# P V of eight head pairs gathered into five blocks per batch, with one copy per block

## The reference, cut to what matters

```python
# x: [32, 256, 128]; 16 heads of 64, 4 persistent key/value rows per head
x = x + attn(layernorm(x))          # rms_norm, q k v, rope, causal softmax, w_out
x = x + ffn(layernorm(x))           # a gated recurrence over the 32 batches, then tanh
# the part of attn around the change:
scores = einsum('bhid,bhjd->bhij', q, k) * scale
attn = softmax(where(causal, scores, min), axis=-1)
out = einsum('bhij,bhjd->bhid', attn, v)     # the product "P V"
out = out.transpose(0, 2, 1, 3).reshape(b, n, heads * dim_head) @ w_out.T
```

## Time and profile before

| | us |
|---|---|
| median of 3 runs | 1124.64 |
| lowest, highest | 1124.19, 1130.9 |
| the profiled execution's own time | 1127.17 |
| its span, first to last instruction | 1125.4 |

### The profile page before, as it was taken

The page is one execution under the profiler, slowest core; times in us unless marked ns, Lnnn a source line. Parts: engine busy times, 40 slices in busy tenths (PEclk is TensorE's granted clock), DMA queues, the critical chain, the costliest instruction groups (busy, mean ns, idle before and its releaser), DMA issues.

```text
span 1125.4 us, 47265 instructions
## 1 busy us (share of the span) xinstructions
PE 1079.8 (96%) x18443; PEld 814.4 (72%) x18443; DVE 934.1 (83%) x3306; ACT 698.1 (62%) x1575; POOL 633.8 (56%) x819
## 2 busy tenths in 40 slices
PE   4979999999999999999999999999999999999996
PEld 2557777777777777777777777777777777777775
DVE  6778888888888888888888888888887889888645
ACT  3746665666666666666666666566675666666634
POOL 4546565556656555665565576565566566656510
PEclk8989999999999999999999999999999999999998
DMA  6222433432333333233333333333332333333215
GB/s 208 105 85 88 115 112 110 120 115 86 95 112 115 116 115 116 78 103 111 116 116 115 108 96 92 111 112 111 115 98 87 113 109 110 111 111 103 71 23 150
DMA packets 78031, 120.52 MB, mean 107 GB/s; under 512 B 13041, under 2 KB 35954, under 8 KB 77682
## 3 DMA queue, kind: packets, MB, share of 16 engines
q1 hardware_dynamic: 68714, 111.20, 32.4%
q10 hardware_dynamic: 9096, 6.30, 2.2%
HBM read 41.56 MB, written 8.78 MB: 45 GB/s over the span
## 4 chain that ended last, share of the span: by engine, by line
PE 66%; DVE 14%; DMA 10%; SPq 3%; issue 3%; POOL 1%; ACT 1%; DVEq 0%; POOLq 0%; ACTq 0%
PE bank_pv L1173 12%; PE bank L1065 12%; PE bank_st L1129 9%; DMA rope_c<-rope_b 7%; PE bank_sum L1210 6%; PE bank_sum L1194 5%; PE bank_sm L1104 4%; DVE masked L835 4%; PE bank L1087 4%; DMA linv_scratch<-linv 3%; PE bank L1084 2%; PE bank L1312 2%; PE bank L1314 2%; PE bank_st L1133 2%; SPq L312 2%
## 5 line engine op out<-in xcount | busy, mean ns | idle before, releaser
L419 POOL TENSOR_TENSOR qk<-rope_a,rope_c 128x512 f32<-128x512 f32 x256 | 341.0, 1332 | 301.2 <-DMA rope_c<-rope_b 293.4
L835 DVE CUSTOM_DVE_ANT_0 masked<-bank_sm,mask_q 128x132 bf16<-128x132 f32 (+1 forms) x1024 | 307.1, 354 | 16.5 <-PE bank_sm L1104 15.7
L412 POOL TENSOR_TENSOR prob<-prob 128x264 f32<-128x264 f32 x256 | 209.5, 818 | 120.0 <-ACT prob L559 113.4
L824 DVE TENSOR_TENSOR rope_a<-bank,cos 128x512 f32<-128x512 f32 x256 | 174.0, 680 | 121.5 <-PE bank L1065 80.7
L544 ACT ACTIVATE qk_h<-qk 128x512 f16<-128x512 f32 x256 | 160.4, 626 | 167.9 <-POOL qk L419 167.2
L559 ACT ACTIVATE prob<-bank_st 128x784 f32<-128x784 f32 x256 | 209.0, 817 | 60.3 <-PE bank_st L1138 59.6
L1173 PE MATMUL bank_pv<-prob,v_sb 128*64 128x256 f32 (+1 forms) x2048 | 224.7, 340 | 0.8 <-DVE raw L851 0.6
L1129 PE MATMUL bank_st<-qk 64*64 64x256 f32 (+3 forms) x4096 | 186.2, 299 | 0.2
L1129 PEld LDWEIGHTS bank_st<-qk 64*64 64x64 f32 x4096 | 167.7, 134 | 9.2 <-issue 0.9
L825 DVE TENSOR_TENSOR rope_b<-bank,sin 128x512 f32<-128x512 f32 x256 | 173.7, 679 | 0.0
L1173 PEld LDWEIGHTS bank_pv<-prob,v_sb 128*64 128x64 f32 x2048 | 124.3, 136 | 54.6 <-issue 1.3
(11 more groups left out here) (241 smaller groups left out, 1738.1 us busy)
## 6 DMA issues: line engine op xcount, KB each, us to landing
rope_c<-rope_b SPq DMA_DIRECT2D x512, 128.0 KB, 2.4
rinv<-linv_scratch SPq DMA_DIRECT2D x124, 256.0 KB, 4.7
out<-x_sb SPq DMA_DIRECT2D x16, 256.0 KB, 3.7
linv_scratch<-linv SPq DMA_DIRECT2D x62, 64.0 KB, 2.0
x_sb<-x ACTq DMA_DIRECT2D x28, 128.0 KB, 5.4
xt<-w_qkv_t ACTq DMA_DIRECT2D x1, 1024.0 KB, 5.4
v_end<-v_end_scratch SPq DMA_DIRECT2D x64, 8.0 KB
v_sb<-pm_v SPq DMA_DIRECT2D x63, 8.0 KB
```

What stands on the lines that cost most here:

```text
L412: G.tensor_tensor(prob_2[:, s % 4, :, :], prob[:, s % 4, :, 0:NT - Q1], prob[:, s % 4, :, C0 + Q1:SCOL], ALU.add).then_inc(S["prob_added"], 1)
L419: G.tensor_tensor(qk[:, s, :].rearrange("p (u n) -> p u n", u=2)[:, :, 0:NT], rope_a[:, (NPAIR * j + s) % 3, :].rearrange("p (u n) -> p u ...
L824: V.tensor_tensor(rope_a[:, (NPAIR * j + s) % 3, :], proj_bank(j, s)[:, :], cos[:, :], ALU.mult)
L835: ins = V.tensor_tensor_reduce(masked[:, e, c0:c0 + n], ps_sm[:, e, c0:c0 + n], mask_q[:, c0:c0 + n], 1.0, LOWEST, ALU.add, ALU.max, top[: ...
```

## The change

P V of a batch is done in five blocks instead of eight. Step 0 has pair 7 with the tail keys, step 2 pairs 0 and 1, step 4 pairs 2 and 3, step 5 pair 4, step 7 pairs 5 and 6. The second pair of a block goes into columns 256 to 511 of the same bank. Only the first pair of a block waits for the copies before it, and ACT makes one copy per block, of 512 or 256 columns. Steps 1, 3 and 6 have no P V any more.

```diff
+PV_AT = {0: (7,), 2: (0, 1), 4: (2, 3), 5: (4,), 7: (5, 6)}
...
-            def raw_copy(bj, par, s):
-                act.wait_ge(S["pv_ready"], NPAIR * bj + s + 1)
+            def raw_copy(bj, par, pairs_of):
+                s, n = pairs_of[0], len(pairs_of)
+                act.wait_ge(S["pv_ready"], NPAIR * bj + s + n)
...
-                A.activation(raw[:, par, s, :], ps_pv[:, 0:NT], ACT.Copy, scale=1.0 / RS).then_inc(S["raw_done"], 1)
+                A.activation(raw[:, par, s:s + n, :].rearrange("p s q -> p (s q)"), ps_pv[:, 0:n * NT], ACT.Copy,
+                             scale=1.0 / RS).then_inc(S["raw_done"], n)
...
                     if s == 0 and c:
-                        raw_copy(j - 2, p, NPAIR - 1)
+                        raw_copy(j - 2, p, PV_AT[0])
...
-                    if s >= 1 and b:
-                        raw_copy(j - 1, 1 - p, s - 1)
+                    if s in (2, 4, 5, 7) and b:
+                        raw_copy(j - 1, 1 - p, PV_AT[s])
...
-            def attend(bj, s):
+            def attend(bj, s, at):
                 pe.wait_ge(S["exp_done"], NPAIR * bj + s + 1)
 
-                wait(pe, S["raw_done"], NPAIR * bj + s)
+                if at == 0:
+                    wait(pe, S["raw_done"], NPAIR * bj + s)
...
-                        last = T.matmul(ps_pv[OWN[e], q0:NT], v_sb[:, kc, col:col + DH], prob[:, s % 4, e, c0:c0 + NT - q0],
+                        last = T.matmul(ps_pv[OWN[e], at + q0:at + NT], v_sb[:, kc, col:col + DH], prob[:, s % 4, e, c0:c0 + NT - q0],
...
                     if s == 0 and c:
-                        attend(j - 2, NPAIR - 1)
-                    if s >= 1 and b:
-                        attend(j - 1, s - 1)
+                        attend(j - 2, NPAIR - 1, 0)
+                    if s in (2, 4, 5, 7) and b:
+                        for i, pair in enumerate(PV_AT[s]):
+                            attend(j - 1, pair, i * NT)
```

## The result

The changed kernel takes 1141.97 us (median; 1141.72 to 1144.06), the kernel before 1127.66 in the four runs beside it. The ratio is 1.0132, 95% interval 1.0089 to 1.0174: slower by a little over one per cent. The prediction was 1142.2 us, 1.56% over the 1124.64 that it started from.

The account below looks back on a forecast made before the run. PE's work seemed the bound, with transpositions waiting for DVE's maxima and the DMA loop only 0.07 us from binding. 0 - 0.07 + 0.65 = +0.58 us per batch, 31 times, less 0.4, gave 1142.2 us; range 1133 to 1150.

Parts of the forecast that it names:

- The step that decided it: Before step 7's transposition: PE, without P V of pair 5, waits 0.8 us uncovered for DVE's maxima of pair 3.
- A second pair at 0.65 us: In a joined P V block: the second pair costs 0.65 us, where a block alone costs 0.81.
- Step 1 to step 3, nothing: From step 1's scores to step 3's transposition: DVE makes these 5.75 us, so joining pairs 0 and 1 changes 0.
- Step 3 to step 7, -0.07: Between the transpositions of steps 3 and 7: joining pairs 2 and 3 saves 0.16, the DMA loop passes only 0.07 us.
- Step 7 to step 1, +0.65: From step 7's transposition to the next step 1's scores: PE bounds these 9.82 us; pair 5's P V adds 0.65.
- The sum: Whole run: +0.58 us per batch, 31 times, with -0.4 for the last batch: +17.6 us, median 1142.2, 1.6% slower.
- The clock: PE's clock through the changed kernel: stays at 1.00 throughout despite a wait of 0.8 us in step 7.
- Faster (1109): Rival, whole kernel: PE's own work is the bound, three joins over 32 batches save 15.4 us; 1109 us, chance 6%.
- About the same (1131): Rival: step 7's 0.8 us wait is real but joins count in full, +0.22 per batch; 1131 us, chance 12%.
- A second pair at 0.81 (1150): Rival, joined P V blocks: a second pair costs as much as a first, 0.81 us; 1150 us, chance 10%.

## Why the prediction was right

**The step that decided it.** "Without the block PE is there at about 588.0 and stands until 588.76, a wait of 0.8 us with no cover": measured 0.73 us, 1.83 us behind the scores as before. The run with pair 5 back removed the loss and the run with pair 5's move alone had all of it.

**A second pair at 0.65 us.** Measured 0.66. Three passages into and out of the 128*64 shape less per batch do save 0.16 us each of PE's own work. The Trainium skill ("TensorEngine Tiling (Array Packing)", "Key Properties") says that a change of the tiling mode drains the engine; if nothing else had changed, the time should have fallen. The trace agrees with the rule, about 0.16 us for coming in and going out together. But pair 5's own 0.66 us went behind a wait that did not get shorter.

**Step 1 to step 3, nothing.** 5.75 us before and after. The join of pairs 0 and 1 turned into 0.19 us of idle PE before the transposition of step 3, where it had been 0.04.

**Step 3 to step 7, -0.07.** This term was sized too small: undisturbed batches took the whole 0.16 us (17.04 to 16.88). The mean over iterations 3 to 31 fell by 0.18, from 17.40 to 17.22. I had let only 0.07 through, from the one batch of the earlier trace rows, and in other batches the exchange lands earlier: from the rotation of pair 5 to the transposition, 11 of the 14 undisturbed batches have 7.4 to 7.9 us, where that batch has 7.35 and DVE's work takes 7.28.

**Step 7 to step 1, +0.65.** Measured 10.39, where from the transposition's start to the scores' start it had been 588.76 to 598.51, or 9.75; the means over iterations 3 to 30 are 10.40 and 9.75, so +0.65.

**The sum.** +0.58 a batch was forecast. Undisturbed batches went from 32.52 to 33.02 between last maxima, +0.50; over iterations 3 to 31 the mean grew by 0.47, or 13.6 us. The forecast has 16.8 for these 29, so it was 3.2 too high there, and nearly all of that is the term from step 3 to step 7 (0.11 a batch). The span grew by 16.9, which seems to agree with the 17.6, but 3.0 of it lie ahead of iteration 3, where the forecast has 0.6. The 2.4 beyond that are not the edit's, as far as the traces tell. In this execution the clock granted to PE rose later than in the one of before, with PE about as busy in the first stretch (5.31 and 5.29 us of 6.00). Stretches of both, the changed kernel first:

```profile
30.00:36.00 6.00, 5.31 (x29) 2.40 (x29) 4.46 (x20) 2.20 (x7) 2.30 (x2) 0.50 0.18 69
36.00:44.00 8.00, 7.61 (x128) 5.10 (x129) 6.35 (x26) 4.69 (x10) 4.15 (x5) 0.82 0.18 68
...
30.00:36.00 6.00, 5.29 (x34) 2.48 (x32) 4.97 (x22) 2.84 (x8) 2.11 (x2) 0.74 0.20 76
36.00:44.00 8.00, 7.89 (x167) 5.74 (x167) 7.26 (x34) 5.61 (x11) 6.29 (x10) 1.00 0.22 82
```

A clock of 0.50 is the lower of PE's two levels, 1.2 GHz, and 1.00 the upper, 2.4 GHz. From the first transposition of step 7 to the scores of the next step 1 PE took 8.57 us in this execution and 6.29 before. The run with two copies, with the same order on PE, had 0.80 and 1.00 in these stretches and took 6.14 us; its first iterations lost 0.3 us in all.

**How much of the number is luck.** The medians grew by 14.3 us (1127.66 to 1141.97), and the forecast was 17.6 on a median of 1124.64 that turned out 3.0 below that of the four runs beside the changed kernel. The growth was 3.3 too high and the start 3.0 too low, and so the forecast of 1142.2 lies 0.2 from the result. The mechanism and its sign do not depend on that, but the closeness does. The ratio, 1.0132, is the better measure: it is below the forecast 1.0156, which its interval holds.

**The clock.** I had argued that it would stay at 1.00 because a wait of 0.8 us was no more than what the stretch of 33.23 us had held. That reading was wrong: the stretch held 33.23 - 32.65 = 0.58 us of idle PE in all. The clock did stay at 1.00 with 0.74 us idle, but my reason for it did not carry that far.

**The rivals.** Faster (1109) was out: the maxima did not come earlier. About the same (1131) was out because the stretch from step 1 to 3 is DVE's: the join there did not count (0.16), nor did the 0.1 for the short wait in step 3. The other two joins did count. A second pair at 0.81 (1150) was out at 0.66.

**What stays open.** Why DMA delays of 2 us hit single batches was not looked into. The worth of the joins by themselves, 2.7 us from the runs with and without two of them, is not clear of the noise in the times; the traces show 0.15 us per undisturbed batch for each join that counts.

## What to carry to other kernels

Before moving work on the bounding engine, ask what it covers: the instruction behind it may be waiting for a result that is exactly as late as the moved work is long, and then the move costs the work once more. An engine that reads as 100% busy can stand at the release of another one at every turn; measure from the start of the producer to the start of the consumer, and see whether that distance is fixed. And look for independent work that can stand ahead of such a wait (here a projection) before saving instructions.

## What the runs showed that I had not expected

Two joins of P V blocks were worth about 3 us together, and one of them, in another setting, cost 17: the version with the earlier reciprocal went from 1130.58 to 1113.77 us by taking two pairs apart. The kernel before, with PE at 96%, gave 6.9 us for the exchange of two neighbouring groups of instructions (ratio 0.9941). And with the reciprocal 1.6 us further forward most batches were alike to 0.01 us, where in the same kernel without that change PE's batches lay between 32.25 and 33.8.
